# Flamingo block: row scores in runs of 512 keys, maxima sent ahead of keys, compact reciprocals, projected values emptied by VectorE

## The chip, the cores and the metric

One core of a Trainium2 chip runs the whole program. The metric is device time in microseconds (us). The kernel before takes 1653.06 us, the median of 3 runs (1650.62 to 1654.22).

Engines are named as the profile does: PE (TensorE matmul), PEld (TensorE weight load), ACT (ScalarE), DVE (VectorE), POOL (GpSimd), SP (SyncE, which here issues every DMA, all on one queue). "b" is a batch entry, "c" a chunk of 512 tokens (two batch entries).

## What is computed

The reference, cut to its core (B=16, S=256, 1601 keys, width 128, 16 heads of depth 8, 8 experts of width 64, top 2):

```python
q = layernorm(x) @ wq.T + bq;  k = ctx @ wk.T + bk;  v = ctx @ wv.T + bv
attn = softmax(q k^T / sqrt(8)) v                       # per head
x = x + tanh(g_xattn) * (attn @ dense.T + dense_b)
n = layernorm(x);  w = top-2 sigmoid gates of n @ gate_W, scaled to sum 1
y = sum_e w_e * (gelu(n @ W1_e + b1_e) @ W2_e + b2_e) + gelu(n @ Ws1 + bs1) @ Ws2 + bs2
x = x + tanh(g_ffn) * y
```

## The kernel before

**Steps.** A step s is one batch entry b = s // 2 and one half of its head pairs (4 pairs, 8 heads). There are 32 working steps, and some before and after. A chunk's feed-forward part is spread over four steps, so the work of the steps repeats with a period of four: phase = s % 4.

**Row scores, "S".** The softmax needs each row's maximum first. `row_scores` computes 128 queries x 401 keys for the two heads of a pair (a matmul each, at rows 0 and 64) into one of two slots `b_ps`, each of two PSUM banks. `maximum` lets DVE reduce the slot. A step has 32 S units: 4 pairs x 2 query tiles x 4 runs of keys. They are computed a step ahead: 12 (`S_AHEAD`) units of step s+2 are already done in step s.

**Maxima, "T".** After a step's last S unit DVE reduces to `neg_max`, PE transposes it (unit T), ACT copies it to `nm_t`, POOL splits it in three bf16 parts (`split3`, four instructions), and `move_maxima` on SP stores these in `m_dram` and loads them as three more rows of `q_op`. From then on the score matmul gives scores minus the maximum.

**Scores and values, "P" and "V".** `score_pair` (L618) computes transposed scores in two of the three banks `a_ps`, ACT takes the exponential (L454), and `values` (L633) multiplies the probabilities by `v_op`, which has 16 columns of ones per head pair, so `o_ps` gets the sums too. A step has 26 P and 13 V units. The first P of a step waits for its maxima (`m_in`).

**Outputs.** `copy_outputs` (L462) takes `o_ps` to `o_s`; `move_outputs` stores it in `o_dram` and loads numerators (`num`) and sums (`den`, every sum repeated for 8 columns). Once per batch entry DVE inverts `den` (128 x 256, L808), POOL multiplies (L422), PE does the dense layer (unit D, L589), and DVE adds it to `x_s`.

**Projections.** K units (four per batch entry, all in the even step, L559) go through `a_ps` to ACT (`k_t`), then POOL splits all 1601 keys in bf16 parts (L392 to L398). `store_keys` stores them with six DMAs (L328), `load_operands` reads them back three steps ahead of use in the operand layout, four DMAs (L279, L281). V units (four per batch entry, in the odd step, L563) go through `a_ps`, and ACT writes `v_op` (L478). Query units QT and QP are in phase 3.

**Feed-forward.** Units FT, FL (phase 1), FG and FH 0 to 4 (phase 2, gelu on ACT at L500 and L502), then FY 0 to 3 (phase 0, L583 to L585: six pairs of a weight load and matmul, the last one the bias `b2s_s` times the gates). DVE normalises (L698) and adds the folded bias (L705). The FH units lie between P units. Where ACT turns from exp to gelu or back, it loads a table: 58 loads in the profile.

**What sets the order.** `PLAN` has one string per phase. PE, ACT and DVE walk through it in the same order, each waiting only for counters. `a_ps` and `b_ps` are rings of 3 and 2. SP's order in a step s is:

```python
load_operands(s + 3); move_outputs(s - 1); spread_gates        # phase 2
load_context(K); store_keys(b + 2)                             # even steps
store_queries; load_context(V)                                 # odd steps
move_maxima(s + 1)
```

POOL's order is: inverse root, gates times `hid`, `attn`, split of the keys (even steps), split of the queries, split of the maxima.

## Time and profile before

| | |
|---|---|
| median of 3 runs | 1653.06 us (1650.62 to 1654.22) |
| the profiled execution | 1659.64 us, of which the span is 1657.9 us |
| busy: PE / DVE / ACT / POOL | 1296.2 / 1102.3 / 1111.1 / 381.7 us |
| mean granted TensorE clock | 0.873 of full speed (2.4 GHz; the lower level is 1.2 GHz) |

The span is what the page measures everything in; the 1.7 us around it belong to the execution. Idle time in a row is that just before the instructions of the group, with the instruction or DMA that ended it.

### The profile page before, as it was taken

How to read it: one execution, taken by the hardware profiler on the slowest of the kernel's cores; microseconds unless marked ns; L12 is line 12 of the kernel's file. 1: busy time of each engine (PE TensorE's matmuls, PEld its weight loads, DVE VectorE, ACT ScalarE, POOL GpSimd, SP SyncE). 2: the span in 40 equal slices, each digit the busy share in tenths (PEclk: the TensorE clock that was granted, in tenths of full speed). 3: DMA queues.
4: the chain of work that ended last, by engine and by line, in shares of the span. 5: the costliest groups of instructions: out<-in, count | busy, mean ns of one | idle time of the engine just before them, and what ended most of it. 6: DMA issues, size and time to landing. Idle time of an engine off the chain costs nothing.

```text
span 1657.9 us, 26852 instructions
## 1 busy us (share of the span) xinstructions
PE 1296.2 (78%) x10019; PEld 461.3 (28%) x10019; DVE 1102.3 (66%) x1459; ACT 1111.1 (67%) x1996; POOL 381.7 (23%) x270
## 2 busy tenths in 40 slices
PE   1377686858897888969899688968899688898765
PEld 0022222222232223323233223323233222332123
DVE  5386586858686677848677586848677585888011
ACT  1016585848885697747977488748977588778741
POOL 6313031130413032030323023130322113000101
PEclk9558898979799798979899797989989797999685
DMA  4962435453643345453443545443543545301001
GB/s 139 192 134 54 99 66 105 103 106 70 134 87 77 84 91 105 84 128 59 117 87 64 109 111 105 85 108 71 124 84 66 111 91 105 66 17 37 11 17 32
DMA packets 66899, 146.42 MB, mean 88 GB/s; under 512 B 9225, under 2 KB 33490, under 8 KB 66770
## 3 DMA queue, kind: packets, MB, share of 16 engines
q1 hardware_dynamic: 66770, 144.72, 41.2%
q8 instruction: 79, 1.29, 0.3%
q14 instruction: 50, 0.41, 0.1%
HBM read 88.04 MB, written 56.65 MB: 87 GB/s over the span
## 4 chain that ended last, share of the span: by engine, by line
PE 53%; ACT 11%; DVE 8%; POOL 7%; issue 7%; DMA 7%; SPq 6%; POOLq 0%; ACTq 0%; DVEq 0%
PE o_ps L633 20%; PE a_ps L618 14%; ACT probs L454 9%; PE b_ps L602 7%; DVE run_max L772 6%; SPq L328 5%; PE a_ps L563 4%; DMA m_dram<-nm_parts 2%; PE a_ps L559 2%; POOL k_t L394 2%; DMA o_dram<-o_s 2%; POOL k_parts L398 2%; POOL k_parts L392 2%; POOL k_parts L396 2%; PE b_ps L583 1%
## 5 line engine op out<-in xcount | busy, mean ns | idle before, releaser
L772 DVE TENSOR_REDUCE run_max<-b_ps 128x2 f32<-128x802 f32 x1024 | 969.6, 988 | 380.9 <-PE b_ps L602 370.0
L454 ACT ACTIVATE probs<-a_ps 128x512 f32<-128x512 f32 (+1 forms) x1664 | 901.0, 594 | 317.5 <-PE a_ps L618 313.2
L618 PE MATMUL a_ps<-q_op,k_op 51*128 51x256 bf16 (+1 forms) x3328 | 346.3, 288 | 246.3 <-ACT probs L454 131.4
L633 PE MATMUL o_ps<-probs,v_op 128*32 128x512 f32 (+1 forms) x3328 | 475.8, 646 | 0.7 <-issue 0.3
L602 PE MATMUL b_ps<-k_op,q_op 48*128 48x401 bf16 x2048 | 348.5, 359 | 51.8 <-DVE run_max L772 27.4
L618 PEld LDWEIGHTS a_ps<-q_op,k_op 51*128 51x128 bf16 (+1 forms) x3328 | 120.1, 98 | 595.1 <-ACT probs L454 415.7
L602 PEld LDWEIGHTS b_ps<-k_op,q_op 48*128 48x128 bf16 x2048 | 100.9, 97 | 312.9 <-DVE run_max L772 237.3
L422 POOL TENSOR_TENSOR attn<-num,den 128x256 f32<-128x256 f32 x16 | 11.6, 727 | 448.8 <-DVE den L808 448.8
L633 PEld LDWEIGHTS o_ps<-probs,v_op 128*32 128x32 f32 (+1 forms) x3328 | 67.2, 111 | 109.9 <-issue 73.1
L392 POOL TENSOR_TENSOR nm_parts<-nm_t,one 8x256 bf16<-8x256 f32 x32 | 19.3, 603 | 333.5 <-ACT nm_t L484 333.5
L756 DVE SCALAR_TENSOR_TENSOR y_s<-b_ps,tgf,x_s 128x128 f32<-128x128 f32 x32 | 11.2, 351 | 116.4 <-PE b_ps L585 116.4
L478 ACT ACTIVATE v_op<-a_ps 128x512 f32<-128x512 f32 x64 | 33.0, 516 | 73.4 <-PE a_ps L563 72.9
L563 PE MATMUL a_ps<-wv_s,vctx 128*128 128x128 f32 (+1 forms) x416 | 78.2, 339 | 0.0
L559 PE MATMUL a_ps<-kctx,wk_s 128*128 128x400 f32 (+1 forms) x128 | 62.6, 581 | 13.7 <-DMA kctx<-ctx_t 13.7
L392 POOL TENSOR_TENSOR k_parts<-k_t,one 128x1601 bf16<-128x1601 f32 x16 | 45.7, 2857 | 105.9 <-ACT k_t L472 92.3
L563 PEld LDWEIGHTS a_ps<-wv_s,vctx 128*128 128x128 f32 (+1 forms) x416 | 63.5, 232 | 23.4 <-issue 15.4
L472 ACT ACTIVATE k_t<-a_ps,bk_s 128x401 f32<-128x401 f32 (+1 forms) x64 | 38.2, 597 | 28.4 <-PE a_ps L559 25.3
L394 POOL TENSOR_TENSOR k_t<-k_t,k_parts 128x1601 f32<-128x1601 f32 x16 | 51.9, 3245 | 1.2
L398 POOL TENSOR_TENSOR k_parts<-k_t,k_parts 128x1601 bf16<-128x1601 f32 x16 | 48.3, 3022 | 1.3
L583 PE MATMUL b_ps<-w_s,hid 128*128 128x128 f32 x256 | 41.5, 311 | 7.2 <-POOL hid L417 7.2
L396 POOL TENSOR_TENSOR k_parts<-k_t,one 128x1601 bf16<-128x1601 f32 x16 | 45.6, 2852 | 1.3
L417 POOL TENSOR_TENSOR hid<-hid,g_all 128x2048 f32<-128x2048 f32 x8 | 36.1, 4517 | 27.5 <-DMA g_all<-g_dram 19.9
(92 smaller groups left out, 694.4 us busy)
## 6 DMA issues: line engine op xcount, KB each, us to landing
k_op<-k_dram SPq DMA_DIRECT2D x64, 600.4 KB, 9.4
k_dram<-k_parts SPq DMA_DIRECT2D x32, 600.4 KB, 7.0
kctx<-ctx_t SPq DMA_DIRECT2D x16, 800.5 KB, 4.6
vctx<-ctx_t SPq DMA_DIRECT2D x16, 800.5 KB, 4.6
k_dram<-k_parts SPq DMA_DIRECT2D x32, 400.2 KB, 7.1
o_dram<-o_s SPq DMA_DIRECT2D x32, 256.0 KB, 7.7
g_all<-g_dram SPq DMA_DIRECT2D x16, 512.0 KB, 5.8
k_dram<-k_parts SPq DMA_DIRECT2D x32, 200.1 KB, 6.7
```

The lines of the kernel that those rows point to most:

```text
L328: sp.dma_start(k_dram[b % 2, a, r0:r1].rearrange("n r c -> r n c"), k_parts[64 * a:64 * a + 64, 0:r1 - r0, :]).then_inc(k_written, 16)
L392: pool.tensor_tensor(parts[0], whole, ones(whole, slice(0, whole.shape[0])), ALU.mult).then_inc(chain, 1)
L394: pool.tensor_tensor(whole, whole, parts[0], ALU.subtract).then_inc(chain, 1)
L396: pool.tensor_tensor(parts[1], whole, ones(whole, slice(0, whole.shape[0])), ALU.mult).then_inc(chain, 1)
L398: pool.tensor_tensor(parts[2], whole, parts[1], ALU.subtract).then_inc(chain, 1)
L454: act.activation(probs[0:keys, unit % PB, :], a_ps[at % AB][0:keys, :], ACT.Exp, scale=SCALE).then_inc(a_taken, 1)
L559: last = pe.matmul(bank[:, 0:n_keys], wk_s[:, :], kctx[:, k0:k0 + n_keys], start=True, stop=True)
L563: last = pe.matmul(bank[0:KEYS[t], 128 * (t % 4):128 * (t % 4) + 128], vctx[:, 128 * t:128 * t + KEYS[t]], wv_s[:, :], start=True, stop=True)
L602: last = pe.matmul(slot[:, side, 0:RUN], q_op[buf][rows, p, 128 * t:128 * t + 128], k_op[buf][rows, p, RUN0[c]:RUN0[c] + RUN], start=True, ...
L618: last = pe.matmul(a_ps[(at + side) % AB][0:KEYS[t], SEQ * a:SEQ * a + SEQ], k_op[buf][rows, slot, 128 * t:128 * t + KEYS[t]], q_op[buf][r ...
L633: pe.matmul(o_ps[32 * j:32 * j + 32, :], v_op[s // 2 % 2][0:KEYS[t], t, GP * (s % 2) + j, :], probs[0:KEYS[t], unit % PB, :], start=(t == ...
L772: dve.tensor_reduce(run_max[:, t, :, p, c:c + 1].rearrange("q v o -> q (v o)"), b_ps[at % BB][:, :, 0:RUN], AX.X, ALU.max).then_inc(b_take ...
```

## The change

The four things of the title, and what comes with them:

- **Runs of 512.** `row_scores` covers 3 full runs of 512 keys; the remaining 65 keys of all four pairs share one slot per query tile. 24 + 2 S units per step in place of 32, `S_AHEAD` 10 in place of 12.
- **Maxima ahead of keys.** POOL splits the maxima before the keys. On SP, `store_keys` moves from the even to the odd step, right behind `move_outputs` and ahead of `load_operands`; both context loads are in the odd step, ahead of `move_maxima`; `store_queries` comes behind it.
- **Compact reciprocals.** `den` is 128 x 32 (each sum once); DVE inverts that, and the new `spread_sums` stores it in `r_dram` and loads it back, repeated, to `den_all`. POOL's `divide` waits for it.
- **Values through `b_ps`.** V units use slots of `b_ps`, DVE empties them. They are spread: 2, 2, 4, 0 over phases 0 to 3.
- **Feed-forward.** The five gelu units stand side by side ("fffff"), with a one-element gelu ahead. The bias rows are joined to `ws2_s` (10 matmul pairs per FY unit, each fp32 product counting two, in place of 12). FY 0 stays in phase 0, FY 1 to 3 go to phase 1, each in two halves. Normalising and adding the bias go from DVE to POOL.
- **Start.** No common barrier: K(0), QT, QP in a prologue; DVE splits the first keys run by run. The loop starts at step -2 in place of -5.

```diff
-RUN = 401
-RUN0 = [400 * i for i in range(4)]
+RUN, RUNS = 512, CTX // 512
+REST = CTX - RUN * RUNS
...
-S_AHEAD = 12
+FULL = GP * QTILES * RUNS
+SUNITS = FULL + QTILES
+S_AHEAD = 10
 PLAN = (
+    "SkSPVSPSkSPVPSkSPVSPvPSSPVPSkSPVPSSPVPSSPVSPdPVPSSPVPSVPTSyPcSPVSPvPSVPSVSP",
+    "vPSVSPyPScPVPSSPVPSSPVPSVSPyPcSPSVPSSPVPSSPVPSfSSPVSPTVSPSfSPVPvSPSVPyPcSPVS",
+    "PVPvPSSPVPVPfSSPVPSkSPVPSkSPVSPvPSkSPVSSPVPdPSSPVPSSPVTSPSVPSkSPVSPSfffffSPSVvPvS",
+    "PqSSPVSPqSPVPSSPVPSSPVPSSPVPSSPVPSSPVPSSPVSSPTVPSSPSPVPSSPVPSSPVSPVP",
 )
...
             for s in range(FIRST, LAST + 1):
                 b = s // 2
+                if 0 <= s - 1 < STEPS:
+                    move_outputs(s - 1)
+                if s % 2 == 1 and b + 2 < BATCH:
+                    store_keys(b + 2)
                 if 0 <= s + 3 < STEPS:
                     load_operands(s + 3)
+                if s % 2 == 0 and 0 <= b - 1 < BATCH:
+                    spread_sums(b - 1)
+                if s % 4 == 2 and 0 <= (s - 6) // 4 < CHUNKS:
+                    spread_gates((s - 6) // 4)
+                if s % 2 == 1 and b + 3 < BATCH:
+                    load_context("K", kctx, b + 3, kctx_in)
+                if s % 2 == 1 and 0 <= b + 2 < BATCH:
+                    load_context("V", vctx, b + 2, vctx_in)
                 if 0 <= s + 1 < STEPS:
                     move_maxima(s + 1)
+                if s % 4 == 3 and 0 < (s + 5) // 4 < CHUNKS:
+                    store_queries((s + 5) // 4)
...
+            def spread_sums(b):
+                sp.wait_ge(den_done, b + 1)
...
+                sp.dma_start(r_dram.rearrange("m s q -> (m s q)").rearrange("(p q) -> p q", q=32),
+                             den[:, :]).then_inc(r_written, 16)
+                sp.wait_ge(r_written, 16 * (b + 1))
...
+                for side in range(2):
+                    sp.dma_start(den_all[64 * side:64 * side + 64, :],
+                                 r_dram[:, side].unsqueeze(1).broadcast_to([2 * GP, DH, SEQ])).then_inc(r_in, 16)
...
+            def load_context(kind, dst, b, arrived):
+                sp.wait_ge(*((a_filled, a_done("K", b - 1, 3)) if kind == "K" else (b_filled, b_done("V", b - 1, 3))))
...
+                if s % 2 == 0 and 0 <= b - 1 < BATCH:
+                    divide(b - 1)
                 if 0 <= s + 1 < STEPS:
+                    split_maxima(s + 1)
+                if s % 2 == 0 and b + 2 < BATCH:
+                    split_keys(b + 2)
...
+            def keep_values(b, i):
...
+                dve.tensor_copy(v_op[b % 2][0:KEYS[t0], t0:t1, :, 0:16],
+                                b_ps[B_SLOT["V", b, i]][0:KEYS[t0], 0, 0:128 * (t1 - t0)]
+                                .rearrange("p (t m c) -> p t m c", t=t1 - t0, c=16)).then_inc(b_taken, 1)
```

In the plan strings k, v, q, f are K, V, query and feed-forward projection units, d the dense layer, y and c the two halves of FY.

## Rows read from the trace of the kernel before

**Rows 1.** Windows, steps 20-23, 13: us, busy PE, PEld, DVE, ACT, POOL, clock, DMA, GB/s.

```profile
1059.30:1116.70 57.40, 41.72 (x335) 16.18 (x332) 33.31 (x39) 30.91 (x58) 15.16 (x9) 0.88 0.46 97
1116.70:1157.00 40.30, 35.89 (x319) 13.79 (x315) 35.47 (x59) 32.75 (x63) 3.54 (x5) 0.96 0.34 69
1157.00:1207.70 50.70, 43.42 (x300) 12.84 (x300) 34.95 (x45) 43.94 (x71) 15.16 (x9) 0.87 0.57 122
1207.70:1247.10 39.40, 35.53 (x308) 13.10 (x306) 31.76 (x42) 31.94 (x60) 12.43 (x10) 0.95 0.41 85
736.80:781.10 44.30, 40.22 (x318) 14.18 (x314) 35.21 (x59) 32.64 (x62) 3.54 (x5) 0.84 0.30 62
```

**Rows 2.** Waits of the whole span: engine and line, releaser, us, times, longest.

```profile
PEld a_ps L618 <- DMA q_op<-m_dram: 118.6, 11, 15.8
```

**Rows 3.** Timeline around the change from step 20 to 21: start, duration, engine, line.

```profile
1094.92 3.02 POOL L398 TENSOR_TENSOR k_parts<-k_t,k_parts 128x1601 bf16<-128x1601 f32 x1
1097.97 9.23 SPq L328 DMA_DIRECT2D k_dram<-k_parts  x6
...
1111.86 0.58 SPq L350 DMA_DIRECT2D q_op<-m_dram  x2
...
1113.76 0.13 PEld L618 LDWEIGHTS a_ps<-q_op,k_op 51*128 51x128 bf16 x4 [14.83 <-DMA q_op<-m_dram]
```

**Rows 4.** Timeline of SP, ends of steps 19 and 21, start of step 22.

```profile
1050.27 0.59 SPq L318 DMA_DIRECT2D vctx<-ctx_t  x1
1050.96 0.30 SPq L347 DMA_DIRECT2D m_dram<-nm_parts  x1
1055.03 0.57 SPq L350 DMA_DIRECT2D q_op<-m_dram  x2
...
1147.33 0.30 SPq L347 DMA_DIRECT2D m_dram<-nm_parts  x1
1148.72 0.57 SPq L350 DMA_DIRECT2D q_op<-m_dram  x2
1153.25 0.32 SPq L279 DMA_DIRECT2D k_op<-k_dram  x1
...
1157.52 0.34 SPq L290 DMA_DIRECT2D o_dram<-o_s  x1
1165.09 0.63 SPq L298 DMA_DIRECT2D num<-o_dram  x1
```

**Rows 5.** Groups by line: count, busy, mean ns, idle before.

```profile
L772 DVE TENSOR_REDUCE run_max<-b_ps 128x2 f32<-128x802 f32 x1024 | 969.6, 988 | 380.9 <-PE b_ps L602 370.0
L563 PE MATMUL a_ps<-wv_s,vctx 128*128 128x128 f32 (+1 forms) x416 | 78.2, 339 | 0.0
L454 ACT ACT_TABLE_LOAD x28 | 35.9, 1283 | 0.5
L583 PE MATMUL b_ps<-w_s,hid 128*128 128x128 f32 x256 | 41.5, 311 | 7.2 <-POOL hid L417 7.2
L584 PE MATMUL b_ps<-ws_s,hid_s 64*128 64x128 f32 x64 | 17.1, 350 | 0.0
L585 PE MATMUL b_ps<-b2s_s,g_t 9*128 9x128 f32 x64 | 17.0, 348 | 0.0
```

**Rows 6.** Timeline of the start.

```profile
44.09 9.21 SPq L328 DMA_DIRECT2D k_dram<-k_parts  x6
57.53 0.35 SPq L279 DMA_DIRECT2D k_op<-k_dram  x1
...
69.45 0.13 PEld L602 LDWEIGHTS b_ps<-k_op,q_op 48*128 48x128 bf16 x4 [20.98 <-DMA q_op<-q_dram]
...
117.72 0.13 PEld L618 LDWEIGHTS a_ps<-q_op,k_op 51*128 51x128 bf16 x4 [2.34 <-DMA q_op<-m_dram]
```

**Rows 7.** Timeline of SP at the end.

```profile
1600.03 0.34 SPq L290 DMA_DIRECT2D o_dram<-o_s  x1
1602.28 0.61 SPq L298 DMA_DIRECT2D num<-o_dram  x1
```

More of the change, by code:

```diff
@@ new lines, with step_of, ring_a, slots_b @@
+PROLOGUE = [("A", ("K", 0, i)) for i in range(4)] + [("A", ("QT", 0, 0)), ("A", ("QP", 0, 0))]
+ORDER = {s: order(s) for s in range(FIRST, LAST + 1)}
+def step_of(unit):
+    return next(s for s in ORDER if any(u == unit for _, u in ORDER[s]))
+def ring_a():
+    at, n = {}, 0
+    for kind, unit in PROLOGUE + [event for s in ORDER for event in ORDER[s]]:
+        if kind in "AP":
+            at[unit] = n
+            n += 2 if kind == "P" else 1
+    return at
+def slots_b():
+    slot, free, own, last, held, n = {}, {}, {}, [0] * BB, None, 0
+    for kind, unit in [event for s in ORDER for event in ORDER[s]]:
+        unit = ("S", unit, 0) if kind == "S" else unit
+        if kind in "SBY":
+            slot[unit] = min((i for i in range(BB) if i != held), key=lambda i: last[i])
+            free[unit] = last[slot[unit]]
+            if kind == "Y":
+                held = slot[unit]
+        if kind in "SBZ":
+            n += 1
+            own[unit] = last[slot[unit]] = n
+        if kind == "Z":
+            held = None
+    return slot, free, own
@@ L379, in _ @@
         def _(pool):
-            for i in range(2):
-                pool.memset(k_op[i][:, :, :], 1.0).then_inc(init, 1)
+            pool.memset(one[:, :], 1.0).then_inc(ones_set, 1)
+            pool.memset(minus_half[:, :], -0.5).then_inc(ones_set, 1)
+            pool.memset(k_op[1][:, :, :], 1.0).then_inc(k_ones[1], 1)
             def ones(like, rows_of=slice(0, 128)):
@@ new lines, in dense, with ffn_output @@
+            def dense(b):
+                slot = b_slot(("D", b, 0))
+                pe.wait_ge(attn_done, b + 1)
+                for t in range(QTILES):
+                    last = pe.matmul(slot[:, 0, 128 * t:128 * t + 128], attn[:, 128 * t:128 * t + 128],
+                                     wd_s[:, :], start=True, stop=True)
+                last.then_inc(b_filled, 1)
+            def ffn_output(c, i, half):
+                tok = slice(128 * i, 128 * i + 128)
+                if half == 0:
@@ L604, in row_scores @@
+                for p, to, k0, n_keys in parts:
+                    for side in range(2):
+                        rows = slice(SIDE * side, SIDE * side + ROWS)
+                        last = pe.matmul(slot[:, side, to:to + n_keys], q_op[buf][rows, p, 128 * t:128 * t + 128],
+                                         k_op[buf][rows, p, k0:k0 + n_keys], start=True, stop=True)
                 last.then_inc(b_filled, 1)
             def score_pair(n):
-                s, i, at = n // SCORE_PAIRS, 2 * (n % SCORE_PAIRS), PLACE["P", n]
+                s, i, at = n // SCORE_PAIRS, 2 * (n % SCORE_PAIRS), A_AT[n]
@@ new lines, in invert_sums @@
+            def invert_sums(b):
+                for h in range(2):
+                    dve.wait_ge(o_in[h], 16 * OUT_DMAS * (b + 1))
+                dve.reciprocal(den[:, :], den[:, :]).then_inc(den_done, 1)
+            dve.memset(k_op[0][:, :, :], 1.0).then_inc(k_ones[0], 1)
+            dve.wait_ge(x0_in, 16)
+            statistics("q", 0)
+            for i in range(len(KRUN)):
+                split_run(i)
+            for i in range(2):
+                dve.memset(v_op[i][:, :, :, 16:32], 1.0).then_inc(v_ones, 1)
```

606 lines of the change are left out of this document (326 added, 280 removed), and 4 rows, old and new, of the table A_UNITS.

## The prediction

> **What bounds the kernel now.** I read the busy times of the four phases first [rows 1]. A cycle of four steps lasts 57.4 + 40.3 + 50.7 + 39.4 = 187.8 us, in which PE is busy for 156.6 us, DVE for 135.6 and ACT for 139.6. PE is the nearest bound, and it isn't the whole answer: phase 0 has 41.7 us of PE work in 57.4 us. Next I read who waited for whom. PE's first scores of a step waited 118.6 us in all for the last DMA of the maxima [rows 2], in 11 places and up to 15.8 us. The timeline shows one such place [rows 3]: POOL ends the split of the keys at 1097.94, SP issues the six key stores until 1107.20, only behind them goes the store of the maxima, and PE starts at 1113.76 after 14.83 us of idleness. Meanwhile PE, ACT and DVE all stand. Without it phase 0 is 57.4 - 14.8 = 42.6 us, 98% PE. So PE's work bounds phase 0, the wait for the keys' traffic ends it, and phases 1 to 3 have gaps of 4 to 7 us each.
>
> The clock matters beside this: step 13, whose TensorE clock was at half speed more (0.84 of full in the mean, against 0.96 in step 21), does the same work in 44.3 in place of 40.3 us, with 40.2 against 35.9 us of PE time [rows 1]. In 44.3 us, 0.12 of clock is 10.6 us more at 1.2 GHz; that cost 4 us.
>
> **Part 1: the wait for the maxima.** POOL now splits the maxima first, and in even steps nothing but small DMAs is left ahead of `move_maxima`. Transposed at P 20 of 26 in phase 0, the maxima need 0.9 us to ACT's copy, about 3.3 us to the store, then 1.4 us from its issue to that of the load (1147.33 to 1148.72) [rows 4] and 1.9 us to PE (1111.86 to 1113.76) [rows 3]: 7.5 us, while 6 P units, a V projection and an FY half last about 11. The waits at the start of odd steps go: up to 118 us.
>
> **But the key stores move to the odd steps.** There I add up SP's queue from the first P of the step:
> - `o_ps` is copied at about +4.7 (3.6 us after PE's restart now, with two S units and QT more ahead); the store of the outputs takes 2.25 us in a free queue [rows 7] and three loads cost 0.65 us of issue each: +9.1.
> - Six key stores, from first issue until all have landed: 57.53 - 44.09 = 13.4 us [rows 6]; the bound below is 9.2, their issue alone [rows 3]. I take 13, as the row of the start measures both ends: +22.1.
> - `load_operands` waits for that. Its first issue at 1153.25, and the outputs' store that was issued behind it at 1157.52 landed at 1165.09 [rows 4]; less 1.4 us for a small store that is 10.5 us: +32.6.
> - Two context loads. With one just ahead the maxima took 4.07 us, without 1.39 [rows 4]: 2.7 us each, +38.0.
> - The maxima, 1.4 + 1.9 us: +41.3.
>
> POOL's key split must be done by +9.1. It takes 12.2 us and starts after the maxima's split at about +37 of a 42 us step 0, so it ends at +7 of phase 1; in phase 2 it ends with the step. So that wait is just covered, and if it weren't, each us would be a us of the odd step.
>
> What would the odd steps take by PE? Phase 3 loses its four V units (78.2 / 16 = 4.9 us [rows 5]): 30.8 us of PE, about 34 with gaps. It would end at +34, the maxima come at +41: **a new wait of 7 us**. Phase 1: 35.9 - 4.9 + 2.45 (two V units) + three FY units; FY costs (41.5 + 17.1) / 32 = 1.83 us without the bias product [rows 5], so 5.5: 39.0 us of PE. It loses the slow clock that a stall of 14.8 us leaves (3 of the 4 us above), and with 7% gaps lasts 38.5; in addition SP waits for the last V unit at P 22 before it issues that context load, about +34, and then 2.7 + 1.4 + 1.9 us give +41. I take 41 for both.
>
> Does the store of the maxima wait for everything ahead? The row shows only one context load ahead of it. The Trainium skill, "DMA: Bandwidth & Descriptors", section "Queues, rings and completion order", says that each DMA engine consumes a queue's descriptors in ring order and that a DMA's semaphore write lands only after all earlier writes of that engine. By it the 12 KB store of maxima waits for the operand loads and both contexts, which is the 41; if only the last load counted, the odd steps would end by PE. No trace here shows the whole pile.
>
> **Part 2: phases 0 and 2.** Phase 0: 41.7 - 4 x 2.36 (FY with bias) + 1.83 + 2.45 = 36.5 us of PE, at 97% 37.7. Ahead of it lie 7 us of wait, which leave a slow clock; for a stall half as long as today's I take 3 us: 40.7. The dense unit waits for a longer chain: outputs stored, sums loaded, DVE inverts at its 10th unit, `r_dram` stored behind the 10.5 us of operand loads and loaded again, POOL multiplies (0.7). From +4.7, with SP still issuing query stores until +6: +9, +13, +14, +23.5, +25.5, +26.4, against a D at P 15, about +25. I take 1.5 us; the bounds are 0 and 8 (today's chain of 9 us for the outputs' store again). Phase 0: 42. Phase 2 has all four V units: 43.4 + 4.9 = 48.3 us of PE. ACT has 43.9 us there now, with most of the 57 loads of 1.283 us between exp and gelu [rows 5]; with the gelus together two per chunk stay, 5.1 x 1.283 = 6.6 us less, and ACT isn't near. 48.3 + 2 of gaps: 50. The gain of the table loads is eaten by the V units that moved in.
>
> For the table loads the Trainium skill's page "ScalarE: Activation LUTs", section "What ACT_TABLE_LOAD costs", adds a drain of 1.38 us to the 1.283: by it the 41 loads would free 109 us of ACT, by the rows 53; PE bounds the phase by either.
>
> **Part 3: VectorE.** Today 802 elements take 988 ns, in rows that overlap to 947 (969.6 / 1024) [rows 5]. At about 1.04 ns for each further element a run of 1024 takes 1.17, one of 520 0.65: 24 x 1.17 + 2 x 0.65 = 29.4 in place of 30.3 us a step. V copies add some 64 x 0.65 = 42 us, reciprocals and normalising take away 50. DVE stays at 34 us of 42: no bound, worth nothing where PE or the queue ends the step. 512-wide matmuls move as many columns as before (25616 against 25664 a step): nothing.
>
> **Part 4: start and end.** Today the keys' stores begin at 44.09, the first S at 69.45, the first P at 117.72 [rows 6]. Without the barrier K(0) can run at 8 to 12 us; DVE splits four runs in about 7.5 us behind its memset: stores at 17, landed at 30 to 32. Context 1, query stores (8 us of issue) and 11.9 us of loads (57.53 to 69.45) [rows 6] give a first S at 49.5. Then 28 S units, 2 V copies and the statistics (36 us) and the way of the maxima behind operand and context loads: first P at 101, 17 us earlier. The end, from the last exponential: the sums' round trip costs 2.5, FY without bias products gains 3 (four pairs at half clock, 0.73 each), statistics come 2.4 earlier, POOL's normalising costs 1 and FY 3 ahead of the gates 2: nothing, within 3.
>
> **Sum** against the profiled execution, by stretches: first P at 101; steps 0 to 3 without feed-forward 42 + 41 + 42 + 41 = 166 (today 303 - 117.7 = 185); steps 4 to 7, without FY, 41 + 41 + 50 + 41 = 173 (today 184.5); five cycles of 42 + 41 + 50 + 41 = 174, 870 (today 944); steps 28 to 31, without keys to store, 39 + 39 + 43 + 36 = 157 (today 166); the rest 61. 101 + 166 + 173 + 870 + 157 + 61 = 1528 us, 1.7 us around it: 1529.7 against 1659.6. The median lies 6.6 us under the profiled execution: 1523 us.
>
> **The rivals.**
> - *PE bounds every step*: the copies overlap, and the odd steps don't wait. Then phases are 38, 38.5, 49, 34: 159.5. Five cycles gain 72 more, the other odd steps (7 + 2) x 4, phase 0's clock 3 each: about 1415 to 1430. For it: DMA share in the windows is at most 0.57 [rows 1]. Against: the chain is serial, three waits for landings, and bytes alone don't shorten it.
> - *The dense unit waits too*: `r_dram` behind the operand loads at the upper bound, 8 us in 16 places against 1.5: +75 (the odd steps get some of it back), about 1598.
> - *Slower than before*: POOL carries a delay over. `divide` waits for the sums' round trip, the maxima's split stands behind it in POOL's queue and the key split behind that; each us by which the keys are split after +9.1 lengthens the odd step. A cycle reaches today's 187.8 us when the odd steps last 48, that is when the split ends at +16, and with the gain of start and first steps used up at +18. At +20 it costs 11 us in each of 14 odd steps: 1523 + 154 = 1677.
> - *It doesn't do what it says*: the maxima end up behind the same stores, one step later, with 14.8 us of wait at each of 14 odd steps: 207 us against the 118 saved, less start: about 1630 to 1665, the edge of no change.
>
> **Chances.** The queue chain in the odd steps 0.53, at 1523 with an own range of 1480 to 1565 (3 us either way in each of 14 odd steps, 2 in the even ones); PE in every step 0.25; dense 0.14; maxima still late 0.04, half of it slower; POOL carry-over 0.04. A measurement of this kernel can tell 0.2%, 3.3 us. Faster 0.92, within 0.02, slower 0.06. The range leaves out the lower end of the second case, the upper half of the third and the last two: 1415 to 1600.
>
> **What would show it.** In the trace of after: the wait of PE for `q_op<-m_dram` is at the end of phase 3 and phase 1, not 0 and 2, some 7 and 2 us; step lengths near 42, 41, 50, 41; on SP the store of the maxima follows the context loads, and its load comes 8 to 12 us later in phase 3; 17 table loads or so; DVE's reduction of 1024 elements at 1.2 us; first S near 50. If phases 1 and 3 are 38 and 34 us with no such wait, the sum of the queue was wrong; if PE waits long at the dense unit, the chain of the sums was.

## The result, and the profile after

The changed kernel takes 1488.9 us in the median of four runs (1480.7 to 1494.7), against 1653.6 us (1650.6 to 1656.4) for the kernel before: a ratio of 0.900, with an interval of 0.896 to 0.905. I had forecast 1523 us, so the gain is 165 us where I said 130. The sign and the mechanism were right, several terms of the sum were not, and their errors partly cancel. Medians and ranges are of fast executions, which leaves out one of the kernel with three mends, 1456.9 us at a granted clock of 0.805 where its others had 0.913 to 0.924.

The profiled execution took 1489.6 us. Its head has the span and the busy time of each engine:

```profile
span 1487.8 us, 26577 instructions
PE 1244.9 (84%) x9955; PEld 431.9 (29%) x9955; DVE 1088.6 (73%) x1272; ACT 1028.5 (69%) x1898; POOL 419.0 (28%) x309
```

The windows of steps 20 to 23 answer to [rows 1], phases 0 to 3 again, each from one copy of `o_s` to the next. The columns are the length, the busy time of PE, PEld, DVE, ACT and POOL, the clock, the DMA share and GB/s:

```profile
944.10:989.40 45.30, 41.14 (x320) 14.82 (x318) 33.08 (x42) 30.75 (x58) 10.97 (x8) 0.85 0.30 56
989.40:1028.50 39.10, 35.69 (x318) 13.49 (x316) 32.79 (x43) 29.55 (x56) 9.80 (x9) 0.97 0.70 159
1028.50:1074.40 45.90, 44.54 (x340) 16.49 (x338) 35.97 (x45) 39.22 (x70) 21.21 (x14) 0.96 0.34 66
1074.40:1112.80 38.40, 32.10 (x276) 8.50 (x274) 30.34 (x28) 28.90 (x56) 9.73 (x9) 0.93 0.72 161
```

The cycle went from 187.8 to 168.7 us. Phase 0 lost 12 us and is still the one with a low clock. Phase 2 lost 5 and is PE to 97%, at clock 0.96 where it had 0.87. Phases 1 and 3 lost 1 us each in these windows (in the means below phase 1 lost 4.1), though they now carry the key stores: their DMA share went from 0.34 and 0.41 to 0.70 and 0.72.

The waits of the whole span (engine and line, releaser, us, times, longest) answer to [rows 2]:

```profile
PEld a_ps L748 <- DMA q_op<-m_dram: 35.9, 15, 3.9
PE b_ps L700 <- POOL attn L506: 44.0, 15, 12.7
PE a_ps L676 <- DMA kctx<-ctx_t: 28.7, 8, 9.4
```

PE waited for the maxima 118.6 us before; now it waits 35.9, in fifteen places of at most 3.9. A second wait is of the same size: the dense unit waits 44.0 us for `attn`. The third is a wait that the kernel before had only once, at its start: the first K unit of a phase 0 stands in the plan ahead of that step's first P, and its context is now loaded in the odd step just before. At the ends of six phases 3 PE waits 2.1 to 4.2 us for that context and then again for the maxima, 5.2 us in the mean of both together. How the maxima wait now is to be read in the timeline of SP over steps 19 and 20 (start, duration, line, tiles, count):

```profile
906.36 0.34 SPq L340 DMA_DIRECT2D o_dram<-o_s  x1
908.43 0.57 SPq L346 DMA_DIRECT2D den<-o_dram  x1
...
910.48 9.43 SPq L394 DMA_DIRECT2D k_dram<-k_parts  x6
924.07 0.33 SPq L329 DMA_DIRECT2D k_op<-k_dram  x1
...
925.86 0.70 SPq L384 DMA_DIRECT2D kctx<-ctx_t  x1
926.60 0.44 SPq L384 DMA_DIRECT2D vctx<-ctx_t  x1
928.14 0.29 SPq L413 DMA_DIRECT2D m_dram<-nm_parts  x1
939.68 0.58 SPq L416 DMA_DIRECT2D q_op<-m_dram  x2
...
953.17 0.38 SPq L329 DMA_DIRECT2D k_op<-k_dram  x1
...
955.91 0.34 SPq L358 DMA_DIRECT2D r_dram<-den  x1
964.71 1.27 SPq L364 DMA_DIRECT2D den_all<-r_dram  x2
...
981.56 0.28 SPq L413 DMA_DIRECT2D m_dram<-nm_parts  x1
982.93 0.57 SPq L416 DMA_DIRECT2D q_op<-m_dram  x2
```

and in PE's rows in the same stretch, where the brackets have the idle time and its releaser:

```profile
941.48 0.13 PEld L748 LDWEIGHTS a_ps<-q_op,k_op 51*128 51x128 bf16 x4 [2.83 <-DMA q_op<-m_dram]
968.92 1.19 PE L700 MATMUL b_ps<-wd_s,attn 128*128 128x128 f32 x4 [3.33 <-POOL attn L506]
```

Step 19 is a phase 3. Its outputs go out at 906.36, the six key stores follow, 13.6 us later (910.48 to 924.07) the operand loads, then both contexts, and the store of the maxima is issued at 928.14. It is only 11.5 us later that the load behind it goes out (939.68). In the even step 20 the same pair takes 1.4 us (981.56 to 982.93). PE stands 2.83 us for the maxima at the end of step 19, and 2.12 just before for the K context, where it stood 14.83 at the end of an even step in [rows 3]. In step 20 `r_dram` is stored at 955.91, behind the operand loads; 8.8 us pass until it can be loaded, and the dense unit comes 3.33 us too late.

To compare kernels I use the mean length of a step in each phase, over steps 8 to 27 of the profiled execution, again from one copy of `o_s` to the next:

| kernel | phase 0 | 1 | 2 | 3 | first P | median us |
|---|---|---|---|---|---|---|
| before | 57.2 | 41.6 | 50.5 | 39.5 | 117.7 | 1653.6 |
| after | 44.8 | 37.5 | 45.6 | 38.4 | 115.2 | 1488.9 |
| keys behind the maxima, alone | 43.6 | 40.6 | 50.4 | 47.1 | 116.1 | 1615.1 |
| whole order of the queues, alone | 41.3 | 38.8 | 49.1 | 38.8 | 112.9 | 1503.8 |
| after, order undone | 54.5 | 38.6 | 64.3 | 34.5 | 103.0 | 1649.4 |
| after, gelus apart | 44.6 | 38.8 | 53.0 | 38.7 | 102.8 | 1535.3 |
| after, runs of 401 keys | 47.2 | 41.2 | 48.5 | 38.0 | 103.1 | 1544.0 |
| after, the same, other places | 45.3 | 39.3 | 45.7 | 37.9 | 104.1 | 1492.7 |
| after, values by ACT | 45.5 | 38.0 | 47.4 | 39.2 | 105.1 | 1499.5 |
| after, wide sums | 40.6 | 39.7 | 46.7 | 39.3 | 102.9 | 1477.2 |
| after, sums first | 39.8 | 38.0 | 45.8 | 38.7 | 102.3 | 1449.2 |
| after, memsets later | 45.0 | 37.7 | 45.5 | 38.4 | 103.2 | 1481.8 |
| after, three mends | 39.2 | 36.1 | 44.4 | 37.0 | 102.0 | 1411.6 |
| the same, values in phase 3 | 40.6 | 35.7 | 44.7 | 35.8 | 101.7 | 1410.3 |

The last column but one is the start of the first P in the profiled execution. The changed kernel's came 10 to 14 us later than that of every kernel built from it, for a reason that is shown below (memsets later). Whether its three other executions paid the same isn't known, so a difference against 1488.9 us can be off by some 12 us. Where it matters I also give the difference from the first P to the end of the span, and the one against the kernel with the memsets later, 1481.8 us.

### The profile page after: what moved, and what is told of

The parts are those of the page before. It is cut to its first block, busy times and chain, and to the rows that moved or that the text cites. A ratio compares the mean times of both kernels' runs of the same rounds, so it can differ in the third digit from the quotient of the medians.

```text
span 1487.8 us, 26577 instructions
## 1 busy us (share of the span) xinstructions
PE 1244.9 (84%) x9955; PEld 431.9 (29%) x9955; DVE 1088.6 (73%) x1272; ACT 1028.5 (69%) x1898; POOL 419.0 (28%) x309
## 3 DMA queue, kind: packets, MB, share of 16 engines
q1 hardware_dynamic: 71250, 145.24, 45.5%
## 4 chain that ended last, share of the span: by engine, by line
PE 54%; DMA 21%; DVE 11%; ACT 6%; SPq 4%; issue 3%; POOL 2%; POOLq 0%; ACTq 0%; DVEq 0%
PE o_ps L763 20%; PE a_ps L748 12%; DMA m_dram<-nm_parts 9%; PE b_ps L732 8%; DVE run_max L896 8%; DMA r_dram<-den 6%; ACT probs L570 4%; PE b_ps L692 3%; DMA den_all<-r_dram 2%; PE a_ps L676 2%; PE b_ps L711 2%; SPq L403 1%; DMA q_op<-m_dram 1%; PE a_ps L672 1%; PE b_ps L700 1%
## 5 line engine op out<-in xcount | busy, mean ns | idle before, releaser
L896 DVE TENSOR_REDUCE run_max<-b_ps 128x2 f32<-128x1024 f32 x768 | 908.4, 1220 | 184.1 <-PE b_ps L732 175.6
L732 PE MATMUL b_ps<-k_op,q_op 48*128 48x512 bf16 (+1 forms) x2048 | 320.2, 351 | 51.6 <-DVE run_max L896 30.9
L732 PEld LDWEIGHTS b_ps<-k_op,q_op 48*128 48x128 bf16 x2048 | 88.3, 95 | 297.4 <-DVE run_max L896 148.6
L506 POOL TENSOR_TENSOR attn<-num,den_all 128x256 f32<-128x256 f32 x16 | 11.6, 725 | 428.4 <-DMA den_all<-r_dram 428.4
L676 PE MATMUL a_ps<-kctx,wk_s 128*128 128x400 f32 (+1 forms) x128 | 73.1, 665 | 35.0 <-DMA kctx<-ctx_t 28.7
L866 DVE COPY v_op<-b_ps 128x512 f32<-128x512 f32 x64 | 37.7, 590 | 49.1 <-PE b_ps L692 46.3
L692 PE MATMUL b_ps<-wv_s,vctx 128*128 128x128 f32 (+1 forms) x416 | 68.2, 308 | 0.9 <-DVE run_max L896 0.5
L692 PEld LDWEIGHTS b_ps<-wv_s,vctx 128*128 128x128 f32 (+1 forms) x416 | 54.9, 204 | 19.8 <-issue 10.4
L700 PE MATMUL b_ps<-wd_s,attn 128*128 128x128 f32 x64 | 13.9, 353 | 44.0 <-POOL attn L506 44.0
L899 DVE TENSOR_REDUCE run_max<-b_ps 128x8 f32<-128x520 f32 x64 | 43.2, 696 | 7.5 <-PE b_ps L732 7.5
L466 POOL TENSOR_TENSOR k_parts<-k_t,one 128x1601 bf16<-128x1601 f32 x15 | 42.8, 2852 | 14.4 <-ACT k_t L591 14.4
L472 POOL TENSOR_TENSOR k_parts<-k_t,k_parts 128x1601 bf16<-128x1601 f32 x15 | 45.3, 3023 | 1.2
```

The costliest lines, as they stand in the source:

```text
L466: pool.tensor_tensor(parts[0], whole, ones(whole, slice(0, whole.shape[0])), ALU.mult).then_inc(chain, 1)
L472: pool.tensor_tensor(parts[2], whole, parts[1], ALU.subtract).then_inc(chain, 1)
L676: last = pe.matmul(bank[:, 0:n_keys], wk_s[:, :], kctx[:, k0:k0 + n_keys], start=True, stop=True)
L692: last = pe.matmul(slot[0:KEYS[t], 0, 128 * (t % 4):128 * (t % 4) + 128], vctx[:, 128 * t:128 * t + KEYS[t]], wv_s[:, :], start=True, stop ...
L732: last = pe.matmul(slot[:, side, to:to + n_keys], q_op[buf][rows, p, 128 * t:128 * t + 128], k_op[buf][rows, p, k0:k0 + n_keys], start=Tru ...
L896: dve.tensor_reduce(run_max[:, t, :, p, c:c + 1].rearrange("q v o -> q (v o)"), slot[:, :, :], AX.X, ALU.max).then_inc(b_taken, 1)
```

## The experiments

### Where the order decides

**The order undone.** The changed kernel, with the six key stores back in the even step ahead of the maxima, and the key split back ahead of theirs on POOL:

```
+                if s % 2 == 0 and b + 2 < BATCH:
+                    store_keys(b + 2)
                 if 0 <= s + 1 < STEPS:
                     move_maxima(s + 1)
-                if s % 2 == 1 and b + 2 < BATCH:
-                    store_keys(b + 2)
```

> The changed kernel with the old order: keys split and stored in the even step, ahead of the maxima. Theory: phase 0 ends 9 us later and phase 2, whose last key projection stands at P 22, some 18 us later, the odd steps lose their waits of 2 to 3 us; 7 x 27 - 14 x 2.5 = 154 us more, with the slow clock behind the stalls 1640 to 1680 us. Rival (the gain came from the other parts): less than 60 us more, under 1550.

Measured: 1649.4 us (1642.2 to 1655.8), 0.998 of before (0.995 to 1.000). The wait is back, larger than before:

```profile
PEld a_ps L748 <- DMA q_op<-m_dram: 188.7, 22, 19.1
```

Everything else of the change was in this kernel, and with the old order it was worth nothing that shows. That isn't what the other parts are worth by themselves: the new plan has its last K unit late in phase 2, so the old order costs more here (188.7 us of wait) than in the kernel before (118.6). Phase 0 got 9.7 us longer and phase 2 by 18.7, as expected. Phase 2 is worst, 64.3 us: in the one around 990 us ACT has copied the maxima at 981.9, POOL splits them only at 997.9, behind the key split, and with the six stores ahead of theirs PE starts again 17.2 us late.

**The order alone, first half.** The kernel before, with its key split behind the maxima's split on POOL and its key stores behind the maxima on SP:

```
-                if s % 2 == 0 and 0 <= b + 2 < BATCH:
-                    store_keys(b + 2)
 ...
                 if 0 <= s + 1 < STEPS:
                     move_maxima(s + 1)
+                if s % 2 == 0 and 0 <= b + 2 < BATCH:
+                    store_keys(b + 2)
```

> The kernel before with one thing of the change: POOL splits the maxima ahead of the keys, and the key stores are issued behind the move of the maxima, at the end of the even step. Theory (the wait of 118.6 us was the order of two queues, and the key stores take some of it back from the odd steps): the waits of 15 us at the starts of odd steps go; SP then stands in the key stores until about +17 of the odd step, outputs and maxima of that step come later, and odd steps get 1 to 3 us longer: 1545 to 1570 us. Rival (the stores only carry the wait on to the next step): 1630 to 1655 us.

Measured: 1615.1 us (1612.4 to 1617.0), 0.976 (0.973 to 0.979). This missed: I had looked for 1545 to 1570. Phase 0 is as short as hoped, 43.6 us, and phase 3 became 47.1. The waits and SP's timeline in phase 3 of this kernel say why:

```profile
PEld a_ps L618 <- DMA q_op<-m_dram: 71.6, 15, 9.8
```

```profile
974.77 9.25 SPq L328 DMA_DIRECT2D k_dram<-k_parts  x6
988.27 0.33 SPq L279 DMA_DIRECT2D k_op<-k_dram  x1
...
990.12 0.69 SPq L290 DMA_DIRECT2D o_dram<-o_s  x1
1000.50 0.68 SPq L298 DMA_DIRECT2D num<-o_dram  x1
...
1003.23 8.61 SPq L337 DMA_DIRECT2D q_dram<-q_parts  x12
1011.88 0.59 SPq L318 DMA_DIRECT2D vctx<-ctx_t  x1
1012.58 0.30 SPq L347 DMA_DIRECT2D m_dram<-nm_parts  x1
1016.73 0.57 SPq L350 DMA_DIRECT2D q_op<-m_dram  x2
```

The stores are out of the way of the even step's maxima, and then the odd step has all of it in one line: keys 13.5 us, the outputs' round trip behind the operand loads 10.4 us (990.12 to 1000.50), twelve query stores 8.6 us, a context, the maxima 4.2 us. PE waited 6.6 us there (it started at 1018.52).

**The order alone, whole.** The same, with the remaining moves of the change on SP but one (the K context stays in the even step): outputs first, key stores next, operand loads behind them, and queries behind the maxima:

```
                 if 0 <= s - 1 < STEPS:
                     move_outputs(s - 1)
+                if s % 2 == 1 and 0 <= b + 2 < BATCH:
+                    store_keys(b + 2)
+                if 0 <= s + 3 < STEPS:
+                    load_operands(s + 3)
 ...
                     move_maxima(s + 1)
+                if s > Q_FIRST and chunk_of(s, Q_FIRST) is not None:
+                    store_queries(chunk_of(s, Q_FIRST))
```

> The kernel before with the changed kernel's whole order on SP and POOL for keys, outputs, queries and maxima: outputs first, key stores in the odd step ahead of the operand loads, query stores behind the maxima. With only the first swap phase 3 took 47.1 us, since outputs (10.4 us behind the operand loads) and query stores (8.6 us) lay ahead of the maxima. Theory (the wait moved down SP's queue, and its length is the sum of what lies ahead): phase 3 comes to 40 us, 7 us less seven times, 1560 to 1575 us. Rival (the rest of that wait is the transfers themselves, whatever their order): 1600 to 1615.

Measured: 1503.8 us (1502.0 to 1507.9), 0.909 (0.907 to 0.912). So the order of two queues, and nothing else, is worth 150 of the 165 us. I had expected 1560 to 1575, since I gave the even steps and phase 3 their share and left phases 1 and 2 as they were; they became 2.8 and 1.4 us shorter too. PE waits for its maxima no longer (0.4 us in one place), nor for a K context after the start, since this kernel loads that in the even step:

```profile
931.14 0.43 SPq L318 DMA_DIRECT2D vctx<-ctx_t  x1
939.01 0.27 SPq L347 DMA_DIRECT2D m_dram<-nm_parts  x1
942.24 0.56 SPq L350 DMA_DIRECT2D q_op<-m_dram  x2
```

From the copy of the outputs (909.49) the store is issued 29.5 us later, where the changed kernel has 22.4, and needs 3.2 us in place of 11.5. The load behind it goes out at 32.8 us against 34.0. PE gets to the next first P only at 37.0 us, where it stood ready at 32.9 in the changed kernel, so the maxima are in time. That the one context less does this is argued, not shown: the kernel with three mends has one context there too, and waits 34.8 us for its maxima.

### The other parts of the change

**Gelus apart.** The five f units that stand together in phase 2 are spread over its exponentials, so ACT changes its table at each:

```
-... PVPdPSSPVPSSPVTSPSVPSkSPVSPSfffffSPSVvPvS
+... PVPdPSSfPVPSSfPVTSPSfVPSkSPVSPfSSfPSVvPvS
```

> The changed kernel with the five gelu units apart again, in four groups among the last score pairs of phase 2: 6 table loads more per chunk, 7.7 us of ACT. Theory (in phase 2 PE has 44.5 us of 45.9, ACT 39.2): ACT comes to 47 us and the phase to about 51: 8 x 5 = 40 us more, 1520 to 1535. Rival (PE bounds phase 2 whatever ACT does, so the grouping was worth nothing): 1489 to 1500.

Measured: 1535.3 us (1533.3 to 1536.5), 0.928 (0.925 to 0.930): 46 us slower than the changed kernel by the medians, 58 us from the first P on. Phase 2 has 7.4 us more in each of its steps, phase 1 has 1.3. Grouping the gelus is worth that. In the changed kernel the groups of table loads (count, busy, mean ns) are down to these, where with the gelus apart there are 57 such loads (28, 21 and 8):

```profile
L585 ACT ACT_TABLE_LOAD x8 | 10.3, 1283 | 0.1
L570 ACT ACT_TABLE_LOAD x7 | 9.0, 1283 | 0.1
```

**Runs of 401 keys.** The changed kernel with the scores in four runs of 401 keys, thus 32 S units a step in place of 26. Each of the six more S units stands beside another S. Over the four phases 14 of the 24 make three S in a row, the other ten two:

```
-RUN, RUNS = 512, CTX // 512
+RUN, RUNS = 401, 4
-    "PqSSPVSPqSPVPSSPVPSSPVPSSPVPSS...
+    "PqSSSPVSPqSPVPSSSPVPSSPVPSSSPVPSS...
```

> The changed kernel with the old runs: four of 401 keys, 32 units per step, 12 ahead, the six more units spread over each plan. Theory (DVE bounds no step): DVE's work grows by about 0.6 us a step, time by 0 to 8 us, 1489 to 1497. Rival (fewer, longer units are what lets PE run ahead): the waits of PE for DVE grow and it costs 20 to 60 us.

Measured: 1544.0 us (1536.0 to 1547.8), 0.932 (0.928 to 0.936), 55 us slower than with 512. That is far more than the DVE time of six units, so I put the same six S units elsewhere, each between a P and a V, where none has another S beside it:

```
-    "PqSSSPVSPqSPVPSSSPVPSSPVPSSSPVPSS...
+    "PqSSPVSPqSPSVPSSPVPSSPSVPSSPVPSSPSVPSS...
```

> As the run with four runs of 401 keys, but the six more units stand between a score pair and a value unit, never beside another S. Theory (each unit takes a slot and PE waits for DVE with each, wherever it stands): 1520 to 1545 us. Rival (only the three S in a row, which two slots can't take, made the 55 us): 1489 to 1505.

Measured: 1492.7 us (1491.1 to 1493.2), 0.902 (0.900 to 0.904), the time of the changed kernel. My own theory for this run, that 32 units cost by their number, fell. The waits of PE for DVE's maxima, of the first and of the second of these kernels:

```profile
PE b_ps L728 <- DVE run_max L891: 161.8, 201, 6.5
```

```profile
PE b_ps L728 <- DVE run_max L891: 62.4, 165, 3.2
```

S writes into one of two slots, and PE takes its units in order. A third S in a row waits for DVE to empty the first, and the P behind it waits too, though nothing holds it. DVE was busy for 71 and 74% of the span in these two kernels. The places of the S units are worth 51 us. How much of that is the three in a row and how much the new pairs wasn't tried apart.

The run length itself shows 4 us in the medians, 14 from the first P on. It costs so little in part because other waits give way: PE waits 62.4 us for DVE's maxima in the second of these kernels and 30.9 in the changed one, but for `attn` only 16.4 in place of 44.0 and for a K context 2.7 in place of 28.7. In a kernel without those waits it wasn't tried.

**Values emptied by ACT.** V units through `a_ps`, emptied by ACT as before, and the rest as changed:

```
-                events.append(("B", ("V", b + 1, n)))
+                events.append(("A", ("V", b + 1, n)))
```

> The changed kernel with the V units through the ring a_ps again and emptied by ACT, at the same places of the plan. 64 copies of 0.59 us leave DVE, 64 of 0.52 come to ACT. Theory (a unit in PE's order costs what its ring makes PE wait; a_ps has three banks that 26 P units keep full, b_ps has slack): 1495 to 1520. Rival (both rings are alike here, only the place in the plan counts): within 5 us of 1489.

Measured: 1499.5 us (1496.6 to 1507.3), 0.908 (0.905 to 0.911). That is 11 us above the changed kernel, 0.7%, and 18 above the kernel with the memsets later; phase 2 is 1.8 us longer, phase 0 by 0.7. So VectorE's slots are the better place, by little: the interval touches that of the changed kernel.

**Wide sums.** No compact reciprocals: SP loads the sums already spread over the rows, DVE inverts 128 x 256, and the round trip through `r_dram` is gone.

```
-                sp.dma_start(den[64 * h:64 * h + 64, :],
-                             od[:, 16, :].rearrange("j (m q) -> j m q", q=32)).then_inc(o_in[h], 16)
+                    sp.dma_start(den[to, :], od[:, 16:24, cols]).then_inc(o_in[h], 16)
```

> The changed kernel with the old sums: den of 128 x 256 loaded in four DMAs, inverted by DVE in 1.75 us, no round trip. Theory (the compact reciprocals cost more in PE's waits for the dense unit than they give DVE): the dense waits of 44 us go, 16 x 1.4 us of DVE come back, and one more DMA issue of 0.65 us lies ahead of the key stores in each odd step: 1455 to 1475. Rival (DVE's time counts, since PE waits for its slots): 1490 to 1510.

Measured: 1477.2 us (1467.2 to 1486.0), 0.893 (0.889 to 0.896), a little faster than the change as it stands (3.8 us from the first P on, 4.6 against the kernel with the memsets later, so hardly more than the scatter). Phase 0 loses 4.2 us, since no store has to pass the operand loads; phases 1 to 3 get longer by 2.2, 1.1 and 0.9 us. That this comes from the longer work on DVE was argued, not shown.

### What still waits

**Sums first.** The changed kernel with one swap on SP, the sums' round trip ahead of the operand loads:

```
+                if s % 2 == 0 and 0 <= b - 1 < BATCH:
+                    spread_sums(b - 1)
                 if 0 <= s + 3 < STEPS:
                     load_operands(s + 3)
-                if s % 2 == 0 and 0 <= b - 1 < BATCH:
-                    spread_sums(b - 1)
```

> The changed kernel, in even steps SP sends the inverted sums ahead of the operand loads. Theory (r_dram takes 8.8 us because 1.4 MB of operand loads are ahead of it, and PE waits for the dense unit 3 to 4 us in phase 0 and about 1 us in phase 2): those waits go, 40 us in sum, with a better clock 1440 to 1460. Rival (phase 0 is set by the way of the maxima, the dense wait is only ahead of another one): 1480 to 1490.

Measured: 1449.2 us (1448.6 to 1451.1), 0.877 (0.874 to 0.879), 40 us less than the changed kernel by the medians. In the two profiles 12.8 of the 40.7 us between them lie ahead of the first P, where the swap changes nothing; 27.9 come after it. Against the kernel with the memsets later, whose first P comes as early, it is 33 us. So one swap is worth some 28 to 33 us, and the 40 that the theory asked for were reached with the help of the start. The dense unit's wait went from 44.0 us in fifteen places to one that matters, at the end of the kernel:

```profile
PE b_ps L700 <- POOL attn L506: 15.9, 4, 12.7
```

Phase 0 lost 5.0 us, more than the 3.8 us of wait in the mean of these steps; the clock of the phase rose too. The window of step 20 of this kernel, to be held against the 41.14 us of PE work at a clock of 0.85 in the changed one:

```profile
916.60:956.62 40.02, 37.79 (x318) 14.04 (x316) 32.85 (x42) 30.69 (x58) 10.94 (x8) 0.95 0.33 63
```

The compact reciprocals are good only with this order: beside it the wide sums are 28 us slower.

**Memsets later.** POOL's two memsets of `k_op` at the start wait until DVE has split the first keys:

```
+            pool.wait_ge(k_first, 4 * len(KRUN))
             for i in (2, 3):
                 pool.memset(k_op[i][:, :, :], 1.0).then_inc(k_ones[i], 1)
```

> The changed kernel, POOL's two memsets of k_op 2 and 3 wait until DVE has split the first keys. In the profile of the changed kernel one DVE cast beside them took 10.50 us in place of 0.37. Theory (POOL and DVE exclude each other there, and the whole start hangs on it): the key stores begin 10 us earlier, the first P too, 1476 to 1482 us where the changed kernel has 1489. Rival (something else sets the first P, or the memsets only move the delay to the operand loads of step 2): 1485 to 1490.

Measured: 1481.8 us (1477.3 to 1487.5), 0.896 (0.893 to 0.899); the interval overlaps that of the changed kernel, so the 7 us aren't proved by the times. The traces show what can be behind them. The start of the changed kernel:

```profile
14.41 0.37 DVE L919 CAST k_parts<-k_t 128x400 bf16<-128x400 f32 x1
...
20.92 10.80 POOL L539 MEMSET k_op<- 128x6404 bf16 x2
21.44 10.50 DVE L919 CAST k_parts<-k_t 128x400 bf16<-128x400 f32 x1
32.58 9.30 SPq L394 DMA_DIRECT2D k_dram<-k_parts  x6
...
115.17 0.13 PEld L748 LDWEIGHTS a_ps<-q_op,k_op 51*128 51x128 bf16 x4 [1.83 <-DMA q_op<-m_dram]
```

and of the kernel with the gelus apart, whose start is the same code:

```profile
18.18 1.20 DVE L919 CAST k_parts<-k_t 128x400 bf16<-128x400 f32 x1
...
20.74 9.36 SPq L394 DMA_DIRECT2D k_dram<-k_parts  x6
...
21.66 10.80 POOL L539 MEMSET k_op<- 128x6404 bf16 x2
...
102.77 0.13 PEld L748 LDWEIGHTS a_ps<-q_op,k_op 51*128 51x128 bf16 x4 [1.82 <-DMA q_op<-m_dram]
```

In the first the last cast began 0.5 us behind the memsets and took 10.50 us, where the same cast took 0.37 just before; the key stores and all behind them came 12 us later. In the second the cast was done before the memsets began. In six more profiles of kernels with this start no such cast stands, and their first P is at 102.3 to 105.1. So one of these eight executions paid some 12 us here. The memsets meet another VectorE instruction in the other seven, the copy of `bv_s` (128 x 128), which takes 7.9 to 9.0 us there and 0.16 in the changed kernel's profile, where it comes behind them; their first P is no later for it. The mended kernel has that too (7.89 us) and its first P at 103.2: the wait makes sure that the cast is never the one.

**Three mends together.** Sums first, memsets later, and the context of K loaded behind the maxima of the even step, so that the odd step has one context ahead of its maxima as in the whole order alone. The last of the three wasn't tried alone.

```
-                if s % 2 == 1 and b + 3 < BATCH:
-                    load_context("K", kctx, b + 3, kctx_in)
 ...
                     move_maxima(s + 1)
+                if s % 2 == 0 and b + 3 < BATCH:
+                    load_context("K", kctx, b + 3, kctx_in)
```

> The changed kernel with the sums ahead of the operand loads, the memsets after the first key split, and the key context loaded at the end of even steps, so that the odd steps have 2.7 us of transfer less ahead of the maxima. Theory (the waits for the maxima, 37 us in 15 places, are the sum of SP's queue in the odd step): most of them go, 1415 to 1430 where the sums alone gave 1449. Rival (PE bounds the odd steps within a us): 1440 to 1450.

Measured: 1411.6 us (1405.8 to 1419.8), 0.854 (0.851 to 0.857), 38 us less than with the sums alone. The time is close to what the theory asked for, but not by its mechanism. Its two waits:

```profile
PEld a_ps L749 <- DMA q_op<-m_dram: 34.8, 15, 4.8
PE a_ps L677 <- DMA kctx<-ctx_t: 1.3, 1, 1.3
```

The waits for the maxima did not go: 34.8 us, where the kernel with the sums first had 36.6. What went is the wait of K units for their context, 22.0 us in eight places there. From the first operand load to the landing of the maxima SP's queue got 2.0 us shorter (872.86 to 886.48 in step 19, 13.6 us in place of 15.6), but without the wait for the context PE comes to the maxima earlier too. The first P is at 102.0, as with the sums first (102.3), so the memsets add nothing to this difference. That wait accounts for part of the 38 us; why phases 1 and 2 also got 1.9 and 1.4 us shorter is open.

**Values in phase 3.** The same, and two of phase 2's four V units moved to phase 3:

```
-... SPSfffffSPSVvPvS   /  PqSSPVSPqSPVPSSPVPSS...
+... SPSfffffSPSVPS     /  PqSSPVSPqSPVvPSSPVvPSS...
```

> As the run before, and two of phase 2's four V units go to phase 3. Theory (phase 2 is bound by PE, 44.5 us of 45.9, phase 3 by SP's queue, 32.1 of 38.4): 2.4 us less in each phase 2 and little more in phase 3, 10 to 20 us under the run before. Rival (with the key context gone from the odd step phase 3 is bound by PE and its exponentials too): the same time within 5 us.

Measured: 1410.3 us (1408.1 to 1420.4), 0.854 (0.851 to 0.857). The rival was right: the 1.3 us between these two are within what they scatter. Phase 2 didn't get shorter with two units less (44.7 against 44.4), so PE did not bind it; phases 1 and 3 lost 0.4 and 1.2 us, phase 0 took 1.4 more. The waits for the maxima fell to 13.2 us. Both kernels beat the one before by 14.6% and the change by 5%. The windows of steps 20 to 23 of this last kernel, as above:

```profile
883.91:926.26 42.35, 37.43 (x318) 14.01 (x316) 32.83 (x42) 30.60 (x58) 10.94 (x8) 0.96 0.39 82
926.26:962.06 35.80, 34.66 (x320) 13.45 (x316) 32.23 (x41) 29.59 (x56) 9.84 (x9) 1.00 0.68 150
962.06:1007.81 45.75, 42.57 (x330) 14.51 (x328) 36.11 (x46) 39.21 (x71) 22.44 (x14) 0.96 0.39 85
1007.81:1043.31 35.50, 33.71 (x286) 9.93 (x284) 30.45 (x29) 29.13 (x54) 8.48 (x9) 0.95 0.71 150
```

The odd steps are PE to 95% and 97% at a clock of 0.95 to 1.00. Phases 0 and 2 are PE to 88% and 93%. The cycle is 159.4 us, and 156.8 in the mean of five; the rival in which PE bounds every step had 159.5, but with 38, 38.5, 49 and 34 for its phases, so that the sums agree is in part luck.

## Why the prediction was right, point by point

- **What bounds the kernel.** Held. The wait for the maxima behind the key stores was the thing to remove: undo that order and all is given back (1649.4), make it alone and 150 of 165 us are there (1503.8).
- **Part 1, the odd steps' queue.** Held as a mechanism, a little too long. From the copy of the outputs to PE's restart I worked out 36.6 us (+4.7 to +41.3); step 19 took 35.8 (905.73 to 941.48). The links: 13.6 us for the key stores against 13, and 15.6 from the first operand load to the landing of the maxima (924.07 to 939.68) against 17.3. What was mis-sized more is the 4.7 us from PE's restart to the copy of the outputs, which took 3.1 (902.56 to 905.73): 3.1 + 35.8 is the 38.9 us from the first P of step 19 to that of step 20, where I had 41. Phase 1 missed by more, 37.5 against 41. There SP's queue waits for the last V unit, and I had that at +34; in step 21 (first P at 987.61) SP issues the context behind it at 1017.47, which is +29.9. From there to PE's restart (1025.91) it is 8.4 us, where I had 6. I had said 7 us of wait in phase 3 and 2 in phase 1. Phase 1 waits 2.4 us for the maxima in the mean, phase 3 2.5; phase 3 stands another 2.9 us in six of its seven places, for the K context. I had counted that load only as traffic ahead of the maxima, and not as something that a unit of the next step waits for. Whether the small store waits for the whole pile was the open point. It does: 11.5 us behind four loads and two contexts, whose last landed at 939.56, 0.1 us before the load behind the store was issued; 4.2 us behind one context (1012.58 to 1016.73), 1.4 in a free queue. By the Trainium skill, "DMA: Bandwidth & Descriptors", section "Queues, rings and completion order", each DMA engine takes a queue's descriptors in ring order and the semaphore's write follows all earlier writes of that engine; the trace agrees.
- **Part 2, phase 0.** The sum said 42 us and the step takes 44.8. The term that was wrong is the dense unit's wait, 1.5 us where 3.3 to 4.2 were measured in six phases 0 (2.0 in the last): D stands at P 15, and I gave PE 25 us until there, though a phase that waits for less reaches it earlier. With the sums ahead the phase takes 39.8 us, so the wait and what it leaves cost 5.0. This was the second rival, with an upper bound of 8 us. Phases 0 waited 24.9 us in all, phases 2 another 6.4, and the swap brought 28 to 33.
- **Part 2, phase 2.** 50 us forecast, 45.6 measured, the largest miss of one step. With the cuts of the forecast, from one first P to the next, the phases 2 up to step 27 took 307 us against 342, 35 us less. I added PE's busy time of before, 43.4 us, to that of the V units, 4.9. That busy time had been read at a clock of 0.87 [rows 1]. Now the clock is 0.96, and PE does the larger phase in 44.5 us. A PE time that is read in a stretch with stalls has the slow clock in it, and must not be carried over to a stretch without. I did allow for this in phases 0 and 1 and forgot it here. I also wrote that the V units eat what the fewer table loads give. They don't: spreading the gelus again costs 7.4 us in each phase 2, 46 to 58 us in all. The drain that the prediction quotes beside a load is not in the rows: in the kernel with the gelus apart an exponential ends at 1072.03, the load takes from 1072.05 to 1073.33, and the next activation starts at 1073.35.
- **Part 3, VectorE.** The reduction of 1024 elements takes 1.22 us in a row, 1.18 by the busy time (908.4 / 768), where I had 1.17; the one of 520 takes 0.70 against 0.65; a V copy 0.59 against 0.65. "Worth nothing" about held for the run length (1492.7 with 401 keys, well placed). It holds only with places that are left between the S units, which I hadn't thought of: the plan's order is worth 51 us.
- **Part 4, start and end.** The first P came at 115.2 in the profiled execution, 14 us later than the 101 of the sum, because of a cast of 10.50 us that I couldn't see in the kernel before; without that collision it comes at 102.3 to 105.1, near the sum. The rest takes 54.9 us against 61. The clock of that stretch is nearly as before, 0.66 against 0.64; PE has 25.8 us of work in it where it had 35.8, and I had counted 3 us of that. The dense unit stands in it for 12.7 us.
- **The sum by stretches.** First P 115.2 against 101; steps 0 to 3 156.6 against 166; steps 4 to 7 169.8 against 173; steps 8 to 27 832 against 870; steps 28 to 31 159 against 157; the rest 54.9 against 61. Up to step 27 the phases 2 are 35 us short of the forecast and the odd steps another 35 (539 against 574), while the phases 0 are 20 over it (313 against 293) and the start 14. So 1523 came within 34 us of 1489 partly by luck: 70 us of error one way stand against 34 the other way.
- **The rivals.** That PE bounds every step was given 1415 to 1430. The change doesn't get there, but the mended kernels do, at 1410 to 1412, by taking away the waits for `attn` and for the K context; PE doesn't bind every step in them either. The third, POOL's delay, didn't show: the key split was done when SP asked for it (908.43 to 910.48 leaves no gap). The fourth, the maxima as late as before, didn't happen; the first half of the order alone comes nearest to it, with its 1615 us. Its price was badly added: 207 us against 118 is 89 us above the kernel before, not 1630 to 1665.

## What to carry to other kernels

A queue has an order as an engine has one: before a large transfer is moved out of the way of a small one, write down everything that the queue holds in the step where it lands, with what each item waits for, and look for the next small transfer that stands behind it. Here half of such a swap brought 38 us, the whole of it 150, and one more swap of the same sort, the sums ahead of the operands, another 28 to 33. A load is to be looked at from both sides: what it keeps waiting behind it in the queue, and who waits for it. And a time that comes out as expected doesn't show the mechanism; the waits by name do, as the three mends showed. And a busy time of TensorE holds only for the clock at which it was read.

## What the runs showed of the hardware

- A DMA of a few kilobytes behind large ones on the same queue waits for all of them: 1.4 us in a free queue, 4.1 to 4.2 behind one context load just issued, 8.8 behind the operand loads, 11.2 behind these and one context (three mends, 875.29 to 886.48), 11.5 behind these and two contexts.
- A cast of 400 elements on VectorE, 0.37 us alone, took 10.50 us when it began 0.5 us behind two GpSimd memsets of 5.4 us each, and ended 0.2 us behind them. VectorE's own memsets of `v_op` took 1.45 us beside the same GpSimd memsets and 1.45 us without them. By the Trainium skill, "SBUF — State Buffer", section "Who interferes with whom", a cast can take the port pair that VectorE shares with GpSimd, and whoever issues first holds it until its instruction ends; the trace agrees. Between the two memsets the cast got no turn, nor did the copy of 128 x 128 that begins beside the first of them in nine other profiles, 7.9 to 9.0 us long; in that of the last kernel it got one, and ended after 1.63 us with the first memset.
- TensorE takes its units in order, and with two result slots it pays for S units that stand side by side, three in a row in 14 places of a cycle and two in ten more: 51 us over the kernel at the same work (1544.0 against 1492.7), with VectorE 71 and 74% busy.
- A busy time of TensorE has the clock of its stretch in it: the sum of 48.3 us for phase 2, from rows at a granted clock of 0.87, was 44.5 us at 0.96.
